# A cross-attention with its softmax products cut into column halves, and its keys split one stage earlier and kept in memory

## The reference

```python
def _L0_ffn_ref(hidden_states, w_up, w_down):      # stage B
    h = hbitlinear(hidden_states, w_up, ACT_BITS)  # Walsh-Hadamard, quantize, product
    h = jnp.square(jax.nn.relu(h))
    out = hbitlinear(h, w_down, ACT_BITS)
...
def _L1_xattn_ref(qkv, y):                         # stage C
    ch = width // N_HEADS                          # 512 // 16 = 32
    q = qkv.reshape(bs * N_HEADS, ch, length)
    k = v = y.reshape(bs * N_HEADS, ch, -1)        # y: 4 x 1601 x 512
    scale = 1.0 / math.sqrt(math.sqrt(ch))
    weight = jnp.einsum('bct,bcs->bts', q * scale, k * scale)
    weight = jax.nn.softmax(weight.astype(jnp.float32), axis=-1)
    a = jnp.einsum('bts,bcs->bct', weight, v)
```

## Time and profile before

| what | value |
|---|---|
| time, median of 3 runs | 1873.78 us (1870.95 to 1878.46) |
| the profiled execution, time | 1874.35 us |
| its span, first to last instruction | 1872.5 us |
| PE, DVE, ACT, POOL busy | 86%, 66%, 43%, 43% |
| stage B | from 469.66 to 702.4 us |
| stage C, from its first score to the end | 748.3 to about 1597 us |

### The profile page before, as it was taken

How to read it: one execution, slowest core, us unless ns; L and a number is a source line. 1 busy time by engine, 2 the same in 40 slices (tenths; PEclk the granted TensorE clock), 3 DMA queues, 4 the chain that set the end, 5 groups by cost and what they waited for, 6 DMA issues and landing times. The chain is left out here.

```text
span 1872.5 us, 22112 instructions
## 1 busy us (share of the span) xinstructions
PE 1619.3 (86%) x7540; PEld 635.7 (34%) x7568; DVE 1240.2 (66%) x1554; ACT 808.1 (43%) x1225; POOL 799.9 (43%) x308
## 2 busy tenths in 40 slices
PE   5999999799677886898888888888888887699898
PEld 2444444344333441222222222222222221344443
DVE  3768999885456558787777777777777740444443
ACT  1321211221443431666666666766666666111110
POOL 0022233543211124666677787676667777000000
PEclk9999999899899995999999999999999999799999
DMA  9232223212211113222211222222212142000000
GB/s 329 71 111 75 82 84 102 82 57 106 68 34 34 26 32 112 72 74 73 74 47 52 63 61 74 75 74 74 61 44 62 44 90 49 1 10 14 22 22 23
DMA packets 136395, 124.36 MB, mean 66 GB/s; under 512 B 61774, under 2 KB 112226, under 8 KB 136294
## 3 DMA queue, kind: packets, MB, share of 16 engines
q1 hardware_dynamic: 131302, 112.56, 21.5%
q10 hardware_dynamic: 4992, 10.49, 1.7%
HBM read 73.49 MB, written 10.76 MB: 45 GB/s over the span
## 5 line engine op out<-in xcount | busy, mean ns | idle before, releaser
L1474 ACT ACTIVATE c_prob<-c_scores,ctx_scales 128x512 f32<-128x512 f32 (+1 forms) x832 | 520.1, 684 | 271.3 <-PE c_scores L1530 265.9
L1374 DVE TENSOR_REDUCE c_piece_max<-c_unit 128x1 f32<-128x804 f32 x512 | 485.4, 984 | 194.3 <-PE c_unit L1513 189.8
L1315 POOL TENSOR_TENSOR c_prob_sum<-c_prob_sum,c_prob 128x2048 f32<-128x2048 f32 x96 | 436.6, 4548 | 16.1 <-ACT c_prob L1474 9.8
L1530 PE MATMUL c_scores<-c_queries,c_keys 97*128 97x512 f16 (+1 forms) x832 | 316.6, 394 | 64.6 <-ACT c_prob L1474 57.3
L1513 PE MATMUL c_unit<-c_khigh,c_qdiag 128*128 128x402 f16 x1024 | 277.0, 354 | 55.1 <-DVE c_piece_max L1374 44.0
L1539 PE MATMUL c_out<-c_prob,c_VT 128*32 128x512 f32 (+1 forms) x1664 | 225.5, 622 | 0.0
L676 PE MATMUL a_S<-a_ctxT,a_xnT 128*128 128x401 f32 x512 | 192.6, 521 | 7.2 <-ACT a_prob L633 3.9
L706 PE MATMUL a_o<-a_ctx,a_probT 128*128 128x512 f32 (+1 forms) x416 | 183.5, 598 | 0.0
L1530 PEld LDWEIGHTS c_scores<-c_queries,c_keys 97*128 97x128 f16 (+1 forms) x832 | 80.0, 99 | 301.9 <-ACT c_prob L1474 232.0
L1513 PEld LDWEIGHTS c_unit<-c_khigh,c_qdiag 128*128 128x128 f16 x1024 | 87.0, 100 | 232.1 <-DVE c_piece_max L1374 131.3
L1315 POOL TENSOR_TENSOR c_prob_sum<-c_prob 128x2048 f32<-128x2048 f32 x16 | 72.6, 4538 | 191.8 <-ACT c_prob L1474 191.8
(11 more groups left out here) (196 smaller groups left out, 1924.3 us busy)
## 6 DMA issues: line engine op xcount, KB each, us to landing
c_k<-in_keys SPq DMA_DIRECT2D x16, 801.0 KB, 6.9
c_keys<-c_khigh SPq DMA_DIRECT2D x128, 100.1 KB, 2.2
a_ctx<-in_ctx SPq DMA_DIRECT2D x12, 1024.0 KB, 6.0
c_VT<-in_values SPq DMA_DIRECT2D x16, 768.0 KB
a_ctxT<-in_ctxT SPq DMA_DIRECT2D x12, 802.0 KB, 4.7
c_keys<-c_krest SPq DMA_DIRECT2D x64, 100.1 KB, 2.2
a_weights<-in_L_ffn_weight SPq DMA_DIRECT2D x3, 1408.0 KB, 14.3
weights_back<-a_weights SPq DMA_DIRECT2D x3, 1408.0 KB, 9.0
```

Of the source, the lines that this page charges most:

```text
L1315: nc.gpsimd.tensor_tensor(psum4[:], a[:], prob[(j * MC + c) % RING][:], ALU.add).then_inc(sums_taken, 2 if i == 1 else 1)
L1374: nc.vector.tensor_reduce(piece_max[j % 2][:, k // 2, k % 2:k % 2 + 1], U[bank(unit)][:, :, 0:PIECE], axis=AX.XY, op=ALU.max).then_inc(uni ...
L1474: nc.scalar.activation(prob[(j * MC + c) % RING][0:w, h, :], STp[h % 2][0:w, :], ACT.Exp, scale=score_scale[0:w]).then_inc(exp_done, 1)
L1530: nc.tensor.matmul(STp[h % 2][0:w, :], K[p][:, h, c * P:c * P + w], Q[p][:, h, :], start=True, stop=True).then_inc(scores_ready, 1)
```

## The change

The products of stage C are cut in two by columns (256 queries each) and placed one piece to a gap, where before a whole block, or up to three, stood in one gap. Two blocks of a slot stay whole: `c_out` of chunk 0 and `c_den` of chunk 4. The last chunk's `c_den` and the block of the sums move to gaps 4 to 7 of the next slot, and VectorE's reciprocals stand before its maxima 3 to 6 of the slot, not 0, 2, 4 and 6. The splitting of the keys leaves stage C: stage B loads them, ScalarE scales and rounds them (four instructions of 801 columns to a group, one to a step), GpSimd subtracts, ScalarE's queue stores both parts in DRAM, and stage C loads them from there, the stacked keys in three DMAs a group (15 DMAs, not 24).

```diff
+            def rest_of_keys(g):
+                pool.wait_ge(khigh_ready, 2 * g + 2)
+                if g > 1:
+                    pool.wait_ge(k_stored[g % 2], 32 * (g // 2))
+                nc.gpsimd.tensor_tensor(krest[g % 2][:], kt[g % 2][:], khigh[g % 2][:], ALU.subtract).then_inc(krest_ready, 1)
...
                 for t in range(ST):
+                    if t == (2 if b > 0 else 0):
+                        rest_of_keys(b * ST)
                     transform(b * ST + t)
+                for g in range(b * ST + 1, (b + 1) * ST):
+                    rest_of_keys(g)
...
+            def load_keys(g):
+                act.dma_start(kt[g % 2][:], keys_dram[g]).then_inc(k_loaded[g % 2], 16)
+
+            def store_keys(g):
+                act.wait_ge(krest_ready, g + 1)
+                for part, k in enumerate((khigh, krest)):
+                    act.dma_start(key_parts_dram[part][g], k[g % 2][:]).then_inc(k_stored[g % 2], 16)
+
+            def split_keys(g, step):
...
+                g, step = divmod(i - KEYS_FROM, KEY_STEPS)
+                if step == 2 and 2 <= g + 1 < G + 1:
+                    store_keys(g - 1)
+                    if g + 1 < G:
+                        load_keys(g + 1)
+                if 0 <= g < G:
+                    split_keys(g, step)
...
+            store_keys(G - 1)
+            for j in range(2):
+                act.wait_ge(k_stored[j], 32 * G // 2)
...
-            def rest_of_k(n, j):
-                dve.wait_ge(khigh_ready, n + 1)
-                wait(dve, stacked, (n - 1) * STACKS)
-                nc.vector.scalar_tensor_tensor(krest[j][:], kt[j][:], key_scale, khigh[j][:], ALU.mult, ALU.subtract).then_inc(krest_ready, 1)
...
-                    if before and u % 2 == 0 and u // 2 < PARTS:
-                        finish(g - 1, u // 2)
+                    if before and 3 <= u < 3 + PARTS:
+                        finish(g - 1, u - 3)
...
+            def placed(before):
+
+                gaps = {}
+                for c in range(1, MC):
+                    for b in {1: [], 2: [0], 3: [1, 2]}.get(c, [c - 1]):
+                        at = 4 * c + (1 if b == c - 1 else 0)
+                        if b == 0:
+                            gaps.setdefault(at + 1, []).append(("out", b, WHOLE))
+                            continue
+                        gaps.setdefault(at, []).append(("out", b, 0))
+                        gaps.setdefault(at + (2 if b not in SUMMED else 1), []).append(("out", b, 1))
+                        if b == SUMMED[0]:
+                            gaps.setdefault(at + 2, []).append(("den", b, WHOLE))
+                        elif b in SUMMED:
+                            gaps.setdefault(at + 2, []).append(("den", b, 0))
+                            gaps.setdefault(at + 3, []).append(("den", b, 1))
+                for half in range(2):
+                    gaps.setdefault(4 * MC + 1 + half, []).append(("out", MC - 1, half))
+                if before:
+                    for i in range(4):
+                        gaps.setdefault(4 + i, []).append(("last", None, i))
+                return gaps
```

More of the change, by code:

```diff
@@ L772, in ffn_0 @@
         gg = [sb(f"b_gg{j}", [P, I]) for j in range(2)]
+        G, MK = keys_dram.shape[0], keys_dram.shape[2]
+        KEYS_FROM, KEY_STEPS = 1, 4
+        key_scale = shared["ctx_scales"][:, 0:1]
+        kt = [sb(f"b_k{j}", [P, MK]) for j in range(2)]
+        khigh = [sb(f"b_khigh{j}", [P, MK], F16) for j in range(2)]
+        krest = [sb(f"b_krest{j}", [P, MK], F16) for j in range(2)]
         Q = 2 * B * ST
@@ L1437, in _ @@
             act.sem_inc(exp_done, EXPS0)
-            def split_keys(n, j):
-                act.wait_ge(k_loaded[j], turn(n, j))
-                if not isinstance(n, int) or n > 1:
-                    act.wait_ge(unit_full, FULL0 + place(n - 2, PAIRS - 1) + 1)
-                    act.wait_ge(stacked, (n - 1) * STACKS)
-                nc.scalar.activation(khigh[j][:], kt[j][:], ACT.Copy, scale=key_scale).then_inc(khigh_ready, 1)
             def split_queries(n, j):
@@ L1464, in exponentials @@
                 for h in range(H):
-                    if c == 0 and h == 2 and (not isinstance(g, int) or g > 0):
+                    if c == 1 and h == 0 and (not isinstance(g, int) or g > 0):
                         take_out(g - 1)
@@ L1488, in slot @@
                         split_queries(g + 2, j % 2)
-                    if c == 2 and more:
-                        split_keys(g + 2, j % 2)
                 if nxt:
@@ L1530, in score, with columns, out @@
                 nc.tensor.matmul(STp[h % 2][0:w, :], K[p][:, h, c * P:c * P + w], Q[p][:, h, :], start=True, stop=True).then_inc(scores_ready, 1)
-            def out(g, j, c):
-                w = P if c < MC - 1 else ML
+            WHOLE = 2
+            def columns(half):
+                return slice(0, D) if half == WHOLE else slice(half * D // 2, (half + 1) * D // 2)
+            def out(g, j, c, half):
+                w, cols = P if c < MC - 1 else ML, columns(half)
                 if c == 0:
@@ L1558, in out_and_den, with den_of_sum @@
-            def out_and_den(g, j, c):
-                last = out(g, j, c)
-                if c in SUMMED:
-                    last = den(g, j, c)
-                last.then_inc(pv_done, 1)
+                if half > 0:
+                    last.then_inc(pv_done, 1)
+            def den_of_sum(g, half):
+                cols = columns(half)
+                if half == 0:
+                    pe.wait_ge(sums_taken, (g + 1) * NP)
+                for h in range(H):
+                    last = nc.tensor.matmul(DEN[h * CH:(h + 1) * CH, cols], ones32[:], psum4[:, h, cols], start=False, stop=half == 1)
+                if half == 1:
+                    last.then_inc(den_done, 1)
@@ L1572, in slot, with products @@
                     return
-                first_gap, gaps = 0, H * MC
-                per_gap = max(len(stream), UNITS) / (gaps - first_gap)
-                gap = given = 0
-                def units():
-                    nonlocal gap, given
-                    gap += 1
-                    upto = round((gap - first_gap) * per_gap)
-                    while given < min(len(stream), upto):
+                before = not isinstance(g, int) or g > 0
+                gaps = placed(before)
+                HALF, PAIR = 0.53, 0.36
+                weights = {gap: sum(HALF * (1 + (what != "last" and half == WHOLE)) for what, b, half in parts) for gap, parts in gaps.items()}
+                per_gap = (sum(weights.values()) + PAIR * max(len(stream), UNITS)) / (H * MC)
+                given, done = 0, 0.0
+                def products(gap):
+                    nonlocal given, done
+                    for what, b, half in gaps.get(gap, []):
+                        if what == "out":
+                            out(g, j, b, half)
+                        elif what == "den":
+                            den(g, j, b, half)
+                        else:
+                            last_sums(g - 1, (j - 1) % TURN, half)
+                        done += HALF * (1 + (what != "last" and half == WHOLE))
+                    upto = (gap - 3) * per_gap
+                    while given < len(stream) and (done + PAIR / 2 <= upto or gap == 4 * MC + 3):
                         unit = stream[given]
-                        if unit[0] == "rows" and upto <= AHEAD + ROWS_AT:
+                        if unit[0] == "rows" and gap < ROWS_GAP:
                             break
@@ L1872, in program @@
         if "B" in stages:
-            ffn_0(nc, shared, bit_weights, had)
+            key_parts = [nc.dram_tensor(f"key_parts{k}", list(keys.shape), F16).ap() for k in range(2)]
+            ffn_0(nc, shared, bit_weights, had, keys, key_parts)
         if "C" in stages:
```

126 lines of the change are left out of this document (65 added, 61 removed).

## The result

The changed kernel takes **1888.84 us** (median of 4 runs, 1887.21 to 1890.99) against 1873.5 before: ratio 1.0079, 95% interval 1.0056 to 1.0103, slower by 0.8%. The forecast was 1865, and "slower" had 0.24.

The account below looks back on a forecast made before the run. The prediction took stage C to be a chain between engines, with ScalarE and VectorE waiting for TensorE's queue. It summed 1874.35 - 47 (stage C) + 38 (stage B) = 1865 us; range 1826 to 1896.

Parts of the forecast that it names:

- slower: Whole kernel: the chance given to a time measurably above the kernel before, 0.24.
- The rest of the keys, -4.1 us a slot: Stage C, VectorE: the rest of the keys leaves, saving 4.1 us in each of 14 slots.
- A half block at 0.67: Stage C, TensorE: a 256-column block costs 0.67 us, 0.43 plus 0.24 for switching; the queue then takes 48.5 a slot.
- `add_gain` waits 4.5, an exponential waits for `c_prob_sum`: Stage C, GpSimd: late reciprocals make `add_gain` wait 4.5 us, delaying chunk 7's first exponential; 1.3 us a slot.
- Two scores wait finished when it comes, and adjacent light and heavy gaps even out: Stage C: reason for charging only 1.3 of 2.0 us for chunk 7's late exponential, giving 49.8 us a slot.
- First and last slot, 3 each: Stage C: the first slot, partly at low clock, and the last, without pairs, gain some 3 us more each.
- Stage B, +38: Stage B: ScalarE's queue waits for key loads and GpSimd's rests; +38 us, 15 if always in time, 55 if every store waits.
- The sum of C: Stage C: 14 slots from 52.7 to 49.8 us give 41, the first and last some 3 each; -47 us.
- The second rival: Stage B loses more than C gains, at `store_keys`, where ScalarE waits for GpSimd: slower, 1884 to 1906, chance 0.22.
- The third rival: Stage C: ScalarE's waits move from blocks to GpSimd's ring, slot stays 51 to 52; 1867 to 1880, chance 0.08.

Follow-up runs that it names:

- e_keys_only: The changed kernel with TensorE's order, the reciprocals' places and the taking out put back as before, blocks whole, only the keys' part kept: 1864.07 us (ratio 0.9945).
- e_even_only: The changed kernel with pairs placed one at a time, evenly over the gaps, rows not held back, `add_gain` left where it was: 1866.90 us (ratio 0.9965).
- e_b_three: The changed kernel with three buffers instead of two for keys, rounded part and rest in stage B, later stores, earlier loads: 1873.00 us (ratio 0.9996).

## Why the prediction was wrong

Its steps, in its order.

- **The rest of the keys, -4.1 us a slot:** near: 4.3 in most slots of `e_keys_only`, 3.7 on their mean.
- **A half block at 0.67:** right, 0.67, and the queue 48.8 for 48.5. The 0.24 us of going into blocks and back is paid by a half as by a whole.
- **`add_gain` waits 4.5, an exponential waits for `c_prob_sum`:** right (4.16, and 3.3 us in two waits). Its price was 1.3 a slot; in the changed kernel 1.2 us stand in the gaps that it lengthens, and 0.8 is what it costs where pairs come evenly.
- **"Two scores wait finished when it comes, and adjacent light and heavy gaps even out": this is the step that failed.** The order was summed as if a gap with two pairs cost 0.22 + 2 x 0.35 wherever it stood. The pace of maxima entered only in the way to the reciprocals; that the new code gives pairs out by weight, two to a gap seven times, and that VectorE (0.93 a maximum, plus reciprocals and moments between) then holds TensorE, has no term. The forecast's slot was 49.8, the measured one 51.0. With nothing changed but the places of the pairs and the rows (`e_even_only`) it is 49.3, the first slot 53.1 us and not 58.4, and the kernel 22 us faster, which is nearly the whole difference between the forecast's 1865 and 1888.84. That it is just this difference is luck in part: the misses below cancel each other, and not all of the 1.7 us is waiting for maxima, as shown above.
- **First and last slot, 3 each:** the first gained nothing. From its first exponential to the next slot's it takes 58.4 us (57.7 before), it has to place 48 pairs, not 32. The last gained more, 8.4: its exponentials take 40.6 us, not 47.3, and the taking out follows 1.9 us after the last one starts, not 3.6.
- **The jump of the loop:** has no term. By the first exponentials its slot is 58.3 with 51.0 beside it, 7.3 us; before it was 54.3 with 53.1 beside it, 1.2.
- **Stage B, +38:** right in sum, +39. At the place shown, from one `rise` to the next but one 573.57 - 557.21 = 16.4 us, forecast 17.4 (568.4 - 551.0), before 10.0. The load wait was 2.40 for 2.6; a rest takes 3.22 for 3.55. What it is made of was off: the forecast had 15 if loads and rests always come in time, and with nearly all of these waits gone (`e_b_three`) the stage still loses 22. Batch by batch the sum was not compared.

The sum of C again, from the first score to the last taking out, with slots counted from first exponential to first exponential. Forecast: 14 slots of 2.9 and 6 at the ends, -47. Measured: twelve full slots from 52.7 to 50.9 on the mean, -21.6; the slot with the jump +4.0; the first slot and the last but one +1.0 together; the last with its taking out -8.4. That is -25.

Of the rivals, none is what happened. Stage B did not lose more than the forecast gave it; stage C gained less. The second rival (stage B loses more) had the direction right, for a reason that did not come true. The third rival's slot ("stays at 51 to 52") came true, but ScalarE's waits moved only in part to GpSimd's ring. The range (1826 to 1896) held the time.

## What to carry to other kernels

When a queue feeds two consumers, sum it with both: a gap takes the greatest of its own work, what the first consumer needs and what the second needs for all it was given lately. Cutting work into more pieces fills slots that another stream was using; look at where that other stream is pushed to. And before moving an instruction to another engine or cutting it, find out what its duration consists of: here three fifths of it was waiting for a neighbour's instruction, which pieces multiply.

## What the runs showed of the hardware

- VectorE's two-input instruction starts only behind the running two-input instruction of GpSimd: 267 columns took 0.47 us alone and 2.95 and 3.42 beside additions of 4.54. The page "SBUF — State Buffer" (SBUF: two separate sides) of the Trainium skill says of the shared port pair that whoever starts first has it for the whole instruction and the other one waits; these times agree. It goes both ways. In the kernel before a rest starts at 1054.82, in an addition that ends at 1057.70, and GpSimd's next instruction on one column takes 1.78 us (median 0.19 in the changed kernel, where VectorE makes no rests in this stage), until the rest has ended:

```profile
1053.17 4.53 POOL L1315 TENSOR_TENSOR c_prob_sum<-c_prob_sum,c_prob 128x2048 f32<-128x2048 f32 x1 [0.16 <-POOL c_prob_sum L1315]
1054.82 4.57 DVE L1383 SCALAR_TENSOR_TENSOR c_krest<-c_k,ctx_scales,c_khigh 128x1602 f16<-128x1602 f32 x1
1057.65 1.78 POOL L1288 TENSOR_TENSOR c_ve<-c_mean_var,c_eps 128x1 f32<-128x1 f32 x1
```

- The jump back of the hardware loop costs TensorE, in the changed kernel, a stretch with nothing to issue: 4.6 us of idle PE and a slower clock behind it, 7.6 us in all. In the other runs with the loop its slot is 1.2 to 8.7 us longer by the first exponentials than those beside it, 1.2 to 2.7 with TensorE's order of before. Written out, the slot shows no stall. What sets its length wasn't tried.
